# First attention: the future part of the diagonal probabilities is cleared on GpSimd, and the steps of a unit follow a table

## The chip, the core and the metric

The kernel runs on one core of one Trainium2 chip. The metric is the time of one execution on the device in microseconds, here of that one core. TensorE multiplies into PSUM, VectorE and ScalarE read PSUM and write on-chip memory (SBUF), GpSimd works in SBUF alone. Each engine runs its own program in order, and the engines meet at semaphores.

## What is computed

A model of four stages on the same tokens: a causal attention, a mixture of experts, a second attention and the experts again. The change is in the first attention only, which is, for 4 batches of 1024 tokens, 16 heads of width 16:

```
q = (x @ Wq.T).reshape(N, L, H, D).transpose(0, 2, 1, 3)     # k and v alike
q = _layernorm(q, gq, bq)                                     # over the 16 of a head
k = _layernorm(k, gk, bk)
scores = jnp.einsum('nhld,nhmd->nhlm', q, k) * SM_SCALE
causal = jnp.tril(jnp.ones((L, L), dtype=bool))
scores = jnp.where(causal, scores, NEG)
attn = jax.nn.softmax(scores, axis=-1)
out = jnp.einsum('nhlm,nhmd->nhld', attn, v)
out = out.transpose(0, 2, 1, 3).reshape(N, L, EMB)
return out @ Wo.T + bo
```

## The kernel before

**Units.** `attention_a` works in 16 units, one for each batch and group of four heads (`UNITS = B * NG`). For a unit all engines do the following steps. `qkv` multiplies normalised tokens by the weights (two halves), ScalarE copies q, k and v out and squares q and k; `spread` sums the squares on VectorE; `norm` finds 1/sqrt on ScalarE (a guess) and GpSimd (one step of refinement, `inverse_root`), and then GpSimd normalises q and k (`normalise`) and writes them with their rounding rest side by side (`build`). `stack` transposes the result on TensorE (four times 8 transposes), and ScalarE copies it out. `max` multiplies q and k of one query tile for two heads, and VectorE takes the maximum of each head: 24 such steps a unit, each two matmuls and two VectorE reductions of up to 512 columns. Four small `peak` steps for each pair of heads turn the maxima into two extra rows of q (L531 to L537), `neg` transposes q again with them (8 transposes, L704), and ScalarE copies that out. `scores` multiplies k and q again, now transposed (keys on the partitions) and with the maximum subtracted by the extra rows; ScalarE takes the exponential from PSUM into `prob`. `values` multiplies `prob` by v into one accumulator (L738), `out` copies it out on ScalarE, `back` transposes it (L747), and VectorE divides by the sum of the row. Every fourth unit `turn` and `project` finish a batch of the output; `stat`, `moments`, `xn` and `tokens` prepare the next batch of tokens.

**Twelve steps of scores.** `STEPS` lists 12 pairs of a block of 512 queries and a tile of 128 keys: tiles 0 to 3 for the first block, 0 to 7 for the second. Eight of the twelve lie on the diagonal (k = 0 to 3 and 8 to 11). There the product is 512, 384, 256 or 128 queries wide, and its first 128 queries include pairs in which the key is in the future. The kernel before adds -1e30 to these in PSUM: after the products of a step, two further bf16 matmuls of an identity with a mask (L726) are accumulated onto the first 128 columns. Of the wide steps there are two halves (one for each pair of heads), each with its own two mask matmuls; that makes 12 halves or steps with a mask in a unit and 24 mask matmuls.

**What sets the order.** One list, `ORDER`, is walked by TensorE, VectorE, ScalarE and GpSimd, each taking from each step what it has to do. `first()` writes the start, `period(n)` writes unit n. Three units are under way in period n: the scores and values of unit n, the maxima of unit n+1, and the projection, normalisation and stacks of unit n+2. `period` lays down the scores of each k with the other steps behind it, then `spread()` deals the maxima evenly over that list up to `end`, and behind `end` follow the stacks with the last two `values` and, last, `("neg", n + 1, 1)`.

**Buffers.** PSUM holds two `wide` slots of 1024 columns (tokens, qkv, stack, neg, scores, turn) that ScalarE empties, three `deep` slots of 512 columns (two for a `max`, one for `back` or `project`) that VectorE empties, and the accumulator. A step of TensorE waits until the use of its slot before has been consumed: a `max` can so start as soon as the first of the two reductions of the `max` before it is done. `prob` has three slots (`PROBS`), so the exponential of step k waits for the `values` of step k-3. GpSimd has nothing to do with `prob` in the kernel before.

Of the kernel before, what the change touches and what calls it, by code (L numbers as in the profile page):

```python
# [110 lines left out]
def attention_a(nc, c, X, tokens_in, W, dram, out, sem):  # L111
# [47 lines left out]
    def xn_tiles(b):  # L159

        return [("xn", b, t) for t in range(TB)]
# [15 lines left out]
    def stacks(u, e):  # L177

        return [("stack", u, 2 * e + i) for i in range(2)] if u < UNITS else []

    def first():

        out = []
        for x in range(2):
            out += [("tokens", 0, x), ("qkv", 0, x), ("spread", 0, x)]
        out += [("norm", 0)] + stacks(0, 0) + stacks(0, 1)
        main = [("qkv", 1, 0), ("spread", 1, 0), ("qkv", 1, 1), ("spread", 1, 1), ("norm", 1)]
        out += spread(main, maxima(0, 0), len(main)) + peak(0, 0)
        main = [("neg", 0, 0)] + stacks(1, 0)
        return out + spread(main, maxima(0, 1), len(main)) + peak(0, 1) + stacks(1, 1) + [("neg", 0, 1)]  # L190

    def period(n):

        b, g = divmod(n, NG)
        more = n + 1 < UNITS
        ahead = n + 2 < UNITS
        main = []
        for k in range(NS):
            main += scores(n, k)
            if ahead and k < 2:  # L200
                main += [("qkv", n + 2, k)]
            if ahead and k in (1, 2):
                main += [("spread", n + 2, k - 1)]
            if ahead and k == 3:
                main += [("norm", n + 2)]
            if k == 1 and n:
                main += [("back", n - 1, 1)]
            if k == TILES + 4:
                main += [("back", n, 0)]
            if k >= 2:  # L210
                main += [("values", n, k - 2)]
            if k == TILES + 1:
                main += [("out", n, 0)]
            if g == 0 and b and k in (5, 7):
                main += [("turn", b - 1, (k - 5) // 2)]
            if g == 0 and b and k in (6, 8):
                main += [("project", b - 1, (k - 6) // 2, i) for i in range(2)]
            if g == 0 and b + 1 < B and k > 1:
                main += moments(b + 1)[k - 2:k - 1]
            if g == 1 and b + 1 < B and k < 4:  # L220
                main += xn_tiles(b + 1)[2 * k:2 * k + 2]
            if g == 1 and b + 1 < B and k in (6, 7):
                main += [("tokens", b + 1, k - 6)]
            if g == 1 and k == 8:
                main += [("bias", b)]
        end = len(main)
        main += stacks(n + 2, 0) + [("values", n, NS - 2)] + stacks(n + 2, 1) + [("values", n, NS - 1), ("out", n, 1)]
        if not more:
            return main
        fill = both_maxima(n + 1)  # L230
        out = spread(main, fill, end)
        at = out.index(("peak", n + 1, 0, 3))
        later = [i for i, s in enumerate(out) if i > at and s[0] == "scores"][2]
        return out[:later] + [("neg", n + 1, 0)] + out[later:] + [("neg", n + 1, 1)]

    ORDER = moments(0) + xn_tiles(0) + first()
    for n in range(UNITS):
# [19 lines left out]
    with ExitStack() as ctx:  # L257
# [56 lines left out]
        s_bias = sem("a_bias_added")  # L314
        s_wide = sem("a_wide_slot_filled")
        s_act = sem("a_wide_slot_consumed")
        s_deep = sem("a_deep_slot_filled")
        s_dve = sem("a_deep_slot_consumed")

# [43 lines left out]
        with nc.Block() as block:  # L363
# [30 lines left out]
            def _(pool):  # L394
# [24 lines left out]
                for step in ORDER:  # L419
                    what = step[0]  # L420
                    if what == "moments" and step[1]:
                        root(step[1])
                    elif what == "norm":

                        u = step[1]
                        pool.wait_ge(s_guess, u + 1)
                        inverse_root(pool, hrstd[:], hvar[:], tmp[:])
                        pool.drain().then_inc(s_hrstd, 1)
                        for side in range(2):
                            if u == 0 and side:  # L430
# [3 lines left out]
                                continue  # L434
                            normalise(pool, side)
                            if side:
                                copied(pool, ("stack", u - 1, 3))
                            elif u > 1:
                                copied(pool, ("neg", u - 2, 1))
                            build(pool, u, side)  # L440
                            pool.drain().then_inc(s_built, 1)
                    elif what == "bias":

                        b = step[1]
                        xs = X[:, b * TB:(b + 1) * TB, :]
                        pool.wait_ge(s_xn, b + 1)
                        pool.tensor_tensor(xs, xs, bo[:].unsqueeze(1).to_broadcast([P, TB, D]), ALU.add)
                        pool.drain().then_inc(s_bias, 1)
# [188 lines left out]
            def _(pe):  # L637
                ident = c["ident"]
                pe.wait_ge(s_init, 1)
                for step in ORDER:  # L640
# [65 lines left out]
                    elif what == "scores":  # L706
# [4 lines left out]
                        diag = kt * P >= qc * QC  # L711
# [1365 lines left out]
```

## Time and profile before

| | |
|---|---|
| median of 3 runs | 4082.97 us (4077.39 to 4085.25) |
| the profiled execution | 4081.54 us |
| its span, first to last instruction | 4079.7 us |
| TensorE busy | 3499.5 us, 86% |
| VectorE / ScalarE / GpSimd busy | 2554.2 / 2217.1 / 1044.8 us |
| first attention, steady part | 103.4 to 912 us of the span |
| TensorE busy in that part | 706.9 of 808.6 us |
| VectorE / ScalarE / GpSimd busy there | 491.7 / 434.4 / 211.0 us |

The span is cut into stretches of time here, and in the first attention a stretch from one second `neg` step to the next is one period. In a timeline of TensorE a line is a run of like matmuls: its start, its length, and in brackets how long the engine had been idle before it and what ended that. Lengths of matmuls are modelled with their way through the array, so they overlap a little: what one costs is the distance from its start to the start of the next. An fp32 matmul of full precision is counted twice (x8 for four of them). Granted clock is TensorE's: 1.00 is 2.4 GHz, 0.50 is 1.2 GHz.

### The profile page before, as it was taken

The numbers are of one execution on the slowest core, as the hardware profiler recorded it, in microseconds if no ns is written. First come the engines' busy times: TensorE is split into PE (matmuls) and PEld (weight loads), VectorE is DVE, ScalarE is ACT, GpSimd is POOL, SyncE is SP. The second block draws the span as 40 slices with busy tenths as digits, with TensorE's granted clock in tenths as the row PEclk, the third lists the DMA queues.
The fourth block names the chain that finished last, engine by engine and source line by source line (L and its number), as shares of the span: only waits on it lengthen the run. The fifth ranks groups of instructions, "written<-read, shape, count | busy, mean of one in ns | idle before, by whom it ended". The sixth has DMA issues, their size and how long they took to land. (4 is left out here: it accounts for less than half of the span.)

```text
span 4079.7 us, 55078 instructions
## 1 busy us (share of the span) xinstructions
PE 3499.5 (86%) x21412; PEld 2544.7 (62%) x21412; DVE 2554.2 (63%) x4350; ACT 2217.1 (54%) x2873; POOL 1044.8 (26%) x924
## 2 busy tenths in 40 slices
PE   4888888888999999996767767777766999999998
PEld 3444454446888889996333333333323888889998
DVE  4666555654443345554999999999996443335564
ACT  1555555554322234442998899889995332224443
POOL 3322223210012201123473272363320002210121
PEclk7889998999999999998777878887777999999999
DMA  3000000001001014332000000000001001012332
GB/s 118 1 1 1 1 1 1 1 1 63 6 24 37 30 41 115 97 89 74 1 1 0 1 1 1 1 1 1 1 1 62 6 7 42 26 49 87 89 93 53
DMA packets 86805, 124.88 MB, mean 31 GB/s; under 512 B 7767, under 2 KB 73257, under 8 KB 86544
## 3 DMA queue, kind: packets, MB, share of 16 engines
q1 hardware_dynamic: 68880, 100.18, 7.3%
q0 software_dynamic: 17664, 21.17, 3.1%
q8 instruction: 170, 2.79, 0.3%
q14 instruction: 91, 0.75, 0.1%
HBM read 85.15 MB, written 42.55 MB: 31 GB/s over the span
## 5 line engine op out<-in xcount | busy, mean ns | idle before, releaser
L1846 DVE TENSOR_TENSOR b_w<-b_w 128x2048 f32<-128x2048 f32 x256 | 583.5, 2310 | 23.9 <-ACT b_w L1924 15.9
L1883 ACT ACTIVATE b_w<-b_ring 128x1024 f32<-128x1024 f32 x512 | 481.8, 1049 | 94.3 <-PE b_ring L1966 93.7
L1924 ACT ACTIVATE b_w<-b_w 128x2048 f32<-128x2048 f32 x256 | 468.1, 1898 | 1.4
L1396 ACT ACTIVATE f2hid<-f2ring 128x512 f32<-128x512 f32 (+2 forms) x256 | 132.6, 518 | 577.4 <-PE f2ring L1476 560.4
L1396 ACT ACTIVATE f1hid<-f1ring 128x512 f32<-128x512 f32 (+2 forms) x256 | 132.6, 518 | 576.6 <-PE f1ring L1476 559.5
L1954 PE MATMUL b_acc<-b_w,b_vg 128*32 128x512 f32 x2048 | 319.9, 705 | 127.8 <-DVE b_w L1846 126.7
L1314 DVE TENSOR_TENSOR f2hid<-f2hid,f2ring 128x512 f32<-128x512 f32 (+2 forms) x256 | 150.1, 586 | 439.7 <-ACT f2hid L1396 439.6
L1314 DVE TENSOR_TENSOR f1hid<-f1hid,f1ring 128x512 f32<-128x512 f32 (+2 forms) x256 | 150.1, 587 | 439.0 <-ACT f1hid L1396 438.9
L620 ACT ACTIVATE a_prob<-a_wide 128x1024 f32<-128x1024 f32 (+1 forms) x320 | 293.0, 944 | 221.5 <-PE a_wide L726 151.8
L518 DVE CUSTOM_DVE_ANT_0 a_deep<-a_deep,a_edge 128x128 f32<-128x128 f32 (+3 forms) x512 | 241.5, 514 | 218.0 <-PE a_deep L696 215.3
L1790 DVE TENSOR_SCALAR b_w<-b_w 128x2048 f32<-128x2048 f32 x256 | 324.8, 1314 | 31.0 <-ACT b_w L1883 30.6
L1476 PE MATMUL f1ring<-f1xh,f1wg 128*128 128x512 f32 (+2 forms) x1536 | 326.1, 354 | 10.6 <-DVE f1xh L1297 8.4
L1476 PE MATMUL f2ring<-f2xh,f2wg 128*128 128x512 f32 (+2 forms) x1536 | 326.1, 354 | 10.1 <-DVE f2xh L1297 7.9
L1966 PE MATMUL b_ring<-b_qT,b_kT 64*128 64x512 f32 x1024 | 237.0, 515 | 101.1 <-ACT b_w L1883 73.3
L1966 PEld LDWEIGHTS b_ring<-b_qT,b_kT 64*128 64x128 f32 x1024 | 94.4, 203 | 317.2 <-ACT b_w L1883 159.8
L1476 PEld LDWEIGHTS f1ring<-f1xh,f1wg 128*128 128x128 f32 x1536 | 250.6, 190 | 35.6 <-DVE f1xh L1297 9.3
L1476 PEld LDWEIGHTS f2ring<-f2xh,f2wg 128*128 128x128 f32 x1536 | 250.7, 190 | 35.1 <-DVE f2xh L1297 8.8
L696 PE MATMUL a_deep<-a_kT,a_qT 64*128 64x512 f32 (+3 forms) x768 | 189.3, 490 | 91.8 <-DVE a_mxp L518 45.6
L1687 POOL CAST b_stacks<-b_qk 128x256 fp32r<-128x256 f32 x64 | 141.5, 2210 | 455.6 <-DVE b_len L1776 444.2
L696 PEld LDWEIGHTS a_deep<-a_kT,a_qT 64*128 64x128 f32 x768 | 80.4, 206 | 244.1 <-DVE a_mxp L518 119.1
L521 DVE TENSOR_REDUCE a_mxp<-a_deep 128x1 f32<-128x512 f32 x256 | 164.7, 685 | 82.2 <-PE a_deep L696 80.5
L1495 PEld LDWEIGHTS f1acc<-f1wd,f1hh 128*128 128x128 f32 x1536 | 200.7, 191 | 17.0 <-DVE f1hh L1142 7.6
(342 smaller groups left out, 7017.5 us busy)
## 6 DMA issues: line engine op xcount, KB each, us to landing
X<-expert_in SPq DMA_DIRECT2D x16, 650.0 KB, 5.0
expert_in<-a_zeros SPq DMA_DIRECT2D x8, 650.0 KB, 10.4
X<-in_x SPq DMA_DIRECT2D x4, 1024.0 KB, 10.0
x_mid<-X SPq DMA_DIRECT2D x8, 512.0 KB, 3.2
f1raw_x<-in_rd SPq DMA_DIRECT2D x4, 1024.0 KB
f1raw_xf<-in_rg SPq DMA_DIRECT2D x4, 1024.0 KB, 4.9
f1raw_xf<-in_ru SPq DMA_DIRECT2D x4, 1024.0 KB, 7.0
f1raw_g<-in_rg SPq DMA_DIRECT2D x4, 1024.0 KB, 4.8
```

The costliest lines, as they stand in the source:

```text
L518: v.tensor_tensor_reduce(got, got, edge[:, CHUNK - n:], 1.0, LOWEST, ALU.add, ALU.max, peak).then_inc(s_dve, 1)
L620: s.activation(dst, src.rearrange("p (h e n) -> p h e n", h=2, e=pairs)[:, :, :, 0:n], ACT.Exp).then_inc(s_act, 1)
L696: last = pe.matmul(dslot(step, h)[:, 0:hi - lo], qT[at, u % 3, e, t * P:(t + 1) * P], kT[at, u % 3, e, lo:hi], start=True, stop=True)
L1314: v.tensor_tensor(hid[:, s % 2, 0:n], hid[:, s % 2, 0:n], slot(step)[:, QC:QC + n], ALU.mult).then_inc(free_of(step), 1)
L1396: s_eng.activation(hid[:, s % 2, 0:n], slot(step)[:, 0:n], ACT.Silu).then_inc(s_silu, 1)
L1476: last = pe.matmul(dst[:, j * QC:j * QC + n], w[:, a, cc, i * P:(i + 1) * P], xh[:, b, x, cc, first:first + n], start=(k == 0 and cc == 0) ...
L1790: v.tensor_scalar(one(m), one(m), LOG_MIN, None, ALU.max).then_inc(s_bound, 1)
L1846: v.tensor_tensor(one(m), one(m), one(m), ALU.mult).then_inc(s_wts, 1)
L1883: s.activation(w[:, m, 2 * pair:2 * pair + 2, :].rearrange("p h n -> p (h n)"), slot(at + pair), ACT.Ln, scale=SHEP_EPS ** -2).then_inc(R. ...
L1924: s.activation(one(m), one(m), ACT.Sigmoid, scale=-0.5).then_inc(s_sig, 1)
L1954: last = pe.matmul(acc[32 * h:32 * h + 32, qc, :], vg[:, u % 2, h, x, :], w[:, x, h, :], start=(x == 0), stop=(x == TB - 1))
L1966: last = pe.matmul(slot(n + e)[:, h * QC:(h + 1) * QC], kT[at, u % 2, e, x * P:(x + 1) * P], qT[at, u % 2, e, qc * QC:(qc + 1) * QC], star ...
```

## The change

All of it is in `attention_a`.

- The mask matmuls are gone. The product of a diagonal step is exponentiated as it is, and then, once the last half of the step is out, GpSimd sets the future entries of the first 128 queries of all four heads in `prob` to zero with one `affine_select` in place (128 partitions by 4 by 128), with a semaphore `s_causal`. The `values` of a diagonal step waits for it too. There are 8 selects a unit.
- `norm` on GpSimd is cut in four parts further on: `("fit", u, side, i)`, i = 0 for `normalise`, i = 1 for `build`. The instructions are the same.
- `spread()` no longer lays out a unit. A table `UNIT` of 95 letters says which kind of step comes next (m a maximum or peak, s scores, v values, q qkv, p spread and norm, w fit, k stack, n neg, b back, o out, x one of the lists of steps that belong to a batch), the same for every unit.

```diff
+    UNIT = ("mbsmxxqmsmmpqxmmsmspvsmspvmswswxvmsvmsommssmmv"
+            "msvmsxwmwsmvmsnmsbxmsvsmkmkxmvmxkmmsmmmvxxkvvo"
+            "xnx")
...
+        for kind in UNIT:
+            if kind == "x":
+                out += aside.pop(0)
+            elif kind == "b" and before:
+                out += before.pop()
+            elif line[kind]:
+                out.append(line[kind].pop(0))
+        return out
...
+                    elif what == "scores":
+
+                        u, k, x = step[1:]
+                        qc, kt = STEPS[k]
+                        n = width(k)
+                        if kt * P >= qc * QC and x == parts(k) - 1:
+                            copied(pool, step)
+                            edges = prob[:, k % PROBS, :, QC - n:QC - n + P]
+                            pool.affine_select(out=edges, in_=edges, compare_op=ALU.is_ge, fill=0.0, base=0,
+                                               pattern=[[0, HG], [1, P]], channel_multiplier=-1)
+                            pool.drain().then_inc(s_causal, 1)
...
-                                                 qT[at, u % 3, e, (qc + 1) * QC - n:(qc + 1) * QC], start=(y == 0),
-                                                 stop=not diag)
-                        if diag:
-                            for h in range(2):
-                                edge = dst[:, h * QC:(h + 1) * QC].rearrange("p (e n) -> p e n", e=pairs)[:, :, 0:P]
-                                last = pe.matmul(edge, c["identb"][:], c["mask_k"][:].unsqueeze(1).to_broadcast([P, pairs, P]),
-                                                 start=False, stop=True)
+                                                 qT[at, u % 3, e, (qc + 1) * QC - n:(qc + 1) * QC], start=True,
+                                                 stop=True)
                         last.then_inc(s_wide, 1)
...
                         copied(pe, ("scores", u, k, parts(k) - 1))
+                        if kt * P >= qc * QC:
+                            pe.wait_ge(s_causal, 2 * TILES * u + qc * TILES + kt % TILES + 1)
```

The order of TensorE at the start of period 7, before (L704 is `neg` of the unit before the seam, L720 `scores`, L726 mask, L696 `max`, L674 `qkv`):

```order
L704 MATMUL a_wide<-ident,a_qs 128x128 x8
L720 MATMUL a_wide<-a_qT,a_kT 128x512 x2
L726 MATMUL a_wide<-mask_k,identb 128x128 x2
L720 MATMUL a_wide<-a_qT,a_kT 128x512 x2
L726 MATMUL a_wide<-mask_k,identb 128x128 x2
L696 MATMUL a_deep<-a_kT,a_qT 128x128 x2
L674 MATMUL a_wide<-a_wqkv,a_xnT 128x192 x8
L696 MATMUL a_deep<-a_kT,a_qT 128x256 x2
L720 MATMUL a_wide<-a_qT,a_kT 128x384 x2
L726 MATMUL a_wide<-mask_k,identb 128x128 x2
```

The same place now (L731 `neg`, L723 `max`, L770 `back`, L746 `scores`, L701 `qkv`):

```order
L731 MATMUL a_wide<-ident,a_qs 128x128 x8
L723 MATMUL a_deep<-a_kT,a_qT 128x128 x2
L770 MATMUL a_deep<-ident,a_oT 128x128 x4
L746 MATMUL a_wide<-a_qT,a_kT 128x512 x2
L723 MATMUL a_deep<-a_kT,a_qT 128x256 x2
L701 MATMUL a_wide<-a_wqkv,a_xnT 128x192 x8
L723 MATMUL a_deep<-a_kT,a_qT 128x384 x2
L746 MATMUL a_wide<-a_qT,a_kT 128x512 x2
L723 MATMUL a_deep<-a_kT,a_qT 128x512 x4
L701 MATMUL a_wide<-a_wqkv,a_xnT 128x192 x8
L723 MATMUL a_deep<-a_kT,a_qT 128x128 x2
```

A `max` and the `back` of the unit before now stand between the `neg` and the first `scores`, the second half of the scores stands behind the first `qkv`, and the masks are gone.

TensorE at the end of period 6, before (L685 `stack`, L738 `values`):

```order
L738 MATMUL a_acc<-a_prob,a_vg 32x384 x4
L685 MATMUL a_wide<-ident,a_qs 128x128 x8
L685 MATMUL a_wide<-ident,a_ks 128x128 x8
L738 MATMUL a_acc<-a_prob,a_vg 32x256 x4
L685 MATMUL a_wide<-ident,a_qs 128x128 x8
L685 MATMUL a_wide<-ident,a_ks 128x128 x8
L738 MATMUL a_acc<-a_prob,a_vg 32x128 x4
L704 MATMUL a_wide<-ident,a_qs 128x128 x8
```

And now (L712 `stack`, L761 `values`; the `stack` before the first row here stands between two `max` as well):

```order
L712 MATMUL a_wide<-ident,a_ks 128x128 x8
L723 MATMUL a_deep<-a_kT,a_qT 128x384 x2
L761 MATMUL a_acc<-a_prob,a_vg 32x512 x4
L723 MATMUL a_deep<-a_kT,a_qT 128x512 x2
L712 MATMUL a_wide<-ident,a_qs 128x128 x8
L723 MATMUL a_deep<-a_kT,a_qT 128x512 x2
L746 MATMUL a_wide<-a_qT,a_kT 128x128 x4
L761 MATMUL a_acc<-a_prob,a_vg 32x384 x4
L712 MATMUL a_wide<-ident,a_ks 128x128 x8
L761 MATMUL a_acc<-a_prob,a_vg 32x256 x4
L761 MATMUL a_acc<-a_prob,a_vg 32x128 x4
L731 MATMUL a_wide<-ident,a_qs 128x128 x8
```

Of the 24 `max` steps none stood in this last part before, behind the last `scores`. Now four stand between the first and the last of the four stacks, and behind the last `max` there are a `scores`, a `values`, a `stack` and two more `values` before the `neg`.

GpSimd from one unit's k (L340 to L344 `normalise`, L356 to L361 `build`) to the next unit's `norm` (L75), before:

```order
L340 TENSOR_TENSOR a_qk<-a_qk,a_hrstd 128x512
L342 TENSOR_TENSOR a_qk<-a_qk,a_gain 128x512
L344 TENSOR_TENSOR a_qk<-a_qk,a_shift 128x512
L356 CAST a_ks<-a_qk 128x32x16 [waits a_wide_slot_consumed]
L357 CAST a_ks<-a_qk 128x32x16
L361 TENSOR_TENSOR a_ks<-a_qk,a_ks 128x32x16
L75 TENSOR_TENSOR a_tmp<-a_hrstd 128x64 [waits a_head_rstd_guessed]
```

And now (L352 to L356 `normalise`, L368 to L373 `build`):

```order
L352 TENSOR_TENSOR a_qk<-a_qk,a_hrstd 128x512
L354 TENSOR_TENSOR a_qk<-a_qk,a_gain 128x512
L356 TENSOR_TENSOR a_qk<-a_qk,a_shift 128x512
L368 CAST a_ks<-a_qk 128x32x16 [waits a_wide_slot_consumed]
L369 CAST a_ks<-a_qk 128x32x16
L373 TENSOR_TENSOR a_ks<-a_qk,a_ks 128x32x16
L466 AFFINE_SELECT a_prob<-a_prob 128x4x128 [waits a_wide_slot_consumed] x8
L75 TENSOR_TENSOR a_tmp<-a_hrstd 128x64 [waits a_head_rstd_guessed]
```

Eight selects (four of the last diagonal steps, four of the first of the next unit) stand between one unit's `build` and the next unit's `norm`; each waits for ScalarE's exponential.

## Rows read from the trace of the kernel before

**Rows 1.** Windows of the first attention: TensorE, its weight loads, VectorE, ScalarE, GpSimd busy; clock.

```profile
103.40:315.10 211.70, 182.52 (x1230) 97.09 (x1228) 131.49 (x403) 113.14 (x154) 59.86 (x70) 0.90 0.00 1
315.10:531.20 216.10, 189.59 (x1285) 104.17 (x1281) 133.26 (x409) 115.44 (x157) 59.89 (x70) 0.92 0.00 1
531.20:752.40 221.20, 195.60 (x1284) 106.19 (x1281) 133.83 (x409) 115.68 (x157) 59.87 (x70) 0.89 0.00 1
752.40:912.00 159.60, 139.18 (x982) 72.91 (x978) 93.09 (x288) 90.10 (x115) 31.33 (x35) 0.96 0.00 1
```

**Rows 2.** Waits of TensorE from 100 to 912 us: total, times, longest.

```profile
PE a_deep L696 <- DVE a_mxp L521: 39.0, 62, 1.3
PE a_deep L696 <- DVE a_mxp L518: 38.1, 67, 1.8
```

**Rows 3.** Timeline of TensorE in period 7: start, length, instructions, idle before.

```profile
483.16 1.09 PE L704 MATMUL a_wide<-ident,a_qs 128*128 128x128 f32 x8
...
485.51 0.51 PE L720 MATMUL a_wide<-a_qT,a_kT 64*128 64x512 f32 x2 [0.62 <-ACT a_qT L611]
485.95 0.29 PE L726 MATMUL a_wide<-mask_k,identb 128*128 128x128 bf16 x2
486.16 0.33 PE L696 MATMUL a_deep<-a_kT,a_qT 64*128 64x128 f32 x2
486.42 2.87 PE L674 MATMUL a_wide<-a_wqkv,a_xnT 128*128 128x192 f32 x16
...
496.52 0.33 PE L696 MATMUL a_deep<-a_kT,a_qT 64*128 64x128 f32 x2 [0.80 <-DVE a_mxp L521]
...
498.04 0.51 PE L696 MATMUL a_deep<-a_kT,a_qT 64*128 64x512 f32 x2 [0.58 <-DVE a_mxp L518]
499.33 0.58 PE L696 MATMUL a_deep<-a_kT,a_qT 64*128 64x256 f32 x2 [0.79 <-DVE a_mxp L521]
499.84 1.94 PE L738 MATMUL a_acc<-a_prob,a_vg 128*32 128x512 f32 x8
...
523.66 0.39 PE L726 MATMUL a_wide<-mask_k,identb 128*128 128x256 bf16 x2
523.99 1.07 PE L738 MATMUL a_acc<-a_prob,a_vg 128*32 128x512 f32 x8
...
531.17 1.09 PE L704 MATMUL a_wide<-ident,a_qs 128*128 128x128 f32 x8
```

**Rows 4.** Two windows of period 7, columns as in Rows 1.

```profile
495.90:499.30 3.40, 1.44 (x10) 0.71 (x10) 2.97 (x10) 1.51 (x2) 0.00 (x0) 1.00 0.00 0
499.30:502.70 3.40, 3.37 (x16) 1.32 (x16) 2.29 (x8) 0.00 (x0) 0.00 (x0) 0.50 0.00 0
```

**Rows 5.** VectorE's groups in period 7: busy us, mean ns, idle before.

```profile
L521 DVE TENSOR_REDUCE a_mxp<-a_deep 128x1 f32<-128x512 f32 x16 | 10.3, 685 | 5.0 <-PE a_deep L696 5.0
L518 DVE CUSTOM_DVE_ANT_0 a_deep<-a_deep,a_edge 128x512 f32<-128x512 f32 x8 | 5.4, 714 | 0.3
L518 DVE DVE_READ_ACCUMULATOR2_ANT a_mxp<- 128x1 f32 x32 | 4.5, 140 | 0.0
L518 DVE CUSTOM_DVE_ANT_0 a_deep<-a_deep,a_edge 128x128 f32<-128x128 f32 x8 | 2.2, 318 | 8.9 <-PE a_deep L696 8.9
```

**Rows 6.** Timeline of GpSimd at the start, in unit 0 and in period 7.

```profile
4.32 0.29 POOL L398 TENSOR_SCALAR_AFFINE_SELECT a_edge<-a_edge 128x128 f32<-128x128 f32 x1 [0.19 <-issue]
...
39.01 1.51 POOL L340 TENSOR_TENSOR a_qk<-a_qk,a_hrstd 128x512 f32<-128x512 f32 x1 [0.24 <-issue]
...
504.33 0.29 POOL L75 TENSOR_TENSOR a_tmp<-a_hrstd 128x64 f32<-128x64 f32 x1 [35.27 <-ACT a_hrstd L602]
...
506.20 1.06 POOL L340 TENSOR_TENSOR a_qk<-a_qk,a_hrstd 128x512 f32<-128x512 f32 x1 [0.24 <-issue]
...
510.23 0.61 POOL L356 CAST a_qs<-a_qk 128x512 fp32r<-128x512 f32 x1
...
518.45 1.29 POOL L361 TENSOR_TENSOR a_ks<-a_qk,a_ks 128x512 f32<-128x512 f32 x1
```

More of the change, by code:

```diff
@@ L179, in stacks, with fits @@
         return [("stack", u, 2 * e + i) for i in range(2)] if u < UNITS else []
+    def fits(u):
+        return [("fit", u, side, i) for side in range(2) for i in range(2)]
     def first():
@@ L185, in first @@
             out += [("tokens", 0, x), ("qkv", 0, x), ("spread", 0, x)]
-        out += [("norm", 0)] + stacks(0, 0) + stacks(0, 1)
-        main = [("qkv", 1, 0), ("spread", 1, 0), ("qkv", 1, 1), ("spread", 1, 1), ("norm", 1)]
-        out += spread(main, maxima(0, 0), len(main)) + peak(0, 0)
+        out += [("norm", 0)] + fits(0) + stacks(0, 0) + stacks(0, 1)
+        main = [("qkv", 1, 0), ("spread", 1, 0), ("qkv", 1, 1), ("spread", 1, 1), ("norm", 1)] + fits(1)
+        out += spread(main, maxima(0, 0), len(main) - 4) + peak(0, 0)
@@ L189, in first, with beside @@
         main = [("neg", 0, 0)] + stacks(1, 0)
         return out + spread(main, maxima(0, 1), len(main)) + peak(0, 1) + stacks(1, 1) + [("neg", 0, 1)]
+    UNIT = ("mbsmxxqmsmmpqxmmsmspvsmspvmswswxvmsvmsommssmmv"
+            "msvmsxwmwsmvmsnmsbxmsvsmkmkxmvmxkmmsmmmvxxkvvo"
+            "xnx")
+    def beside(b, g):
+        at = [[] for _ in range(NS)]
+        if g == 0 and b:
+            for k, step in ((4, ("turn", b - 1, 0)), (5, ("project", b - 1, 0, 0)), (6, ("project", b - 1, 0, 1)),
+                            (6, ("turn", b - 1, 1)), (7, ("project", b - 1, 1, 0)), (8, ("project", b - 1, 1, 1))):
+                at[k].append(step)
+        if g == 0 and b + 1 < B:
+            for k, step in enumerate(moments(b + 1)):
+                at[k + 1].append(step)
+        if g == 1 and b + 1 < B:
+            for i, step in enumerate(xn_tiles(b + 1)):
+                at[i // 2].append(step)
+            at[6].append(("tokens", b + 1, 0))
+            at[8].append(("tokens", b + 1, 1))
+        if g == 1:
+            at[9].append(("bias", b))
+        return at
@@ L192, in period @@
     def period(n):
-        b, g = divmod(n, NG)
         more = n + 1 < UNITS
         ahead = n + 2 < UNITS
[L197 to L234, printed above, removed]
+        line = {
+            "s": [step for k in range(NS) for step in scores(n, k)],
+            "v": [("values", n, k) for k in range(NS)],
+            "o": [("out", n, x) for x in range(2)],
+            "b": [("back", n, 0)],
+            "m": both_maxima(n + 1) if more else [],
+            "n": [("neg", n + 1, e) for e in range(PAIRS)] if more else [],
+            "q": [("qkv", n + 2, x) for x in range(2)] if ahead else [],
+            "p": [("spread", n + 2, 0), ("spread", n + 2, 1), ("norm", n + 2)] if ahead else [],
+            "w": fits(n + 2) if ahead else [],
+            "k": stacks(n + 2, 0) + stacks(n + 2, 1),
+        }
@@ L236, in attention_a @@
+        before = [[("back", n - 1, 1)]] if n else [[]]
+        aside = beside(*divmod(n, NG))
+        out = []
+        for kind in UNIT:
[6 more added lines that the diff above has]
+        return out
     ORDER = moments(0) + xn_tiles(0) + first()
@@ L316, in attention_a @@
         s_act = sem("a_wide_slot_consumed")
+        s_causal = sem("a_future_probs_cleared")
         s_deep = sem("a_deep_slot_filled")
@@ L428, in _ @@
                         pool.drain().then_inc(s_hrstd, 1)
-                        for side in range(2):
-                            if u == 0 and side:
+                    elif what == "fit":
+                        u, side, i = step[1:]
+                        if u == 0 and side:
+                            if i:
                                 pool.wait_ge(s_first, 1)
                                 pool.drain().then_inc(s_built, 1)
-                                continue
+                        elif i == 0:
                             normalise(pool, side)
+                        else:
                             if side:
@@ L710, in _ @@
                         n = width(k)
-                        diag = kt * P >= qc * QC
                         pairs = PAIRS // parts(k)
```

## The prediction

> **What bounds the kernel now.** I read the windows first. In the first attention TensorE is busy 182.5 of 211.7 us, 189.6 of 216.1, 195.6 of 221.2 and 139.2 of 159.6, and VectorE, next in line, 131 to 134 us of each of the first three [rows 1]. So TensorE sets the pace, yet it idles 808.6 - 706.9 = 101.7 us of this part. The second thing to see there is the granted clock: 0.90, 0.92, 0.89 and 0.96. The clock has the two levels 1.2 and 2.4 GHz, so a mean of 0.90 is 20% of the time at 1.2 GHz, and work done there takes twice as long. The loss is about 0.10 x 211.7 + 0.08 x 216.1 + 0.11 x 221.2 + 0.04 x 159.6 = 69 us.
>
> Who causes the idle time stands in the waits: 39.0 + 38.1 = 77 us of it is a `max` of TensorE that waits for VectorE to empty a deep slot [rows 2]. The timeline of period 7, 48.0 us from one `neg` to the next, shows how that comes about and what it brings. Three waits of 0.80, 0.58 and 0.79 us lie within 3.6 us, because `spread` and `back` stand on VectorE between two `max`; right behind them the products of a `values` take 1.94 us where the same eight take 1.07 us later [rows 3]. The windows of these stretches tell the same: TensorE is busy 1.44 of 3.4 us while VectorE is busy 2.97, and the 3.4 us after that are granted 0.50 [rows 4]. At the end of the period the picture is turned round: there is no `max` behind the last `scores`, and VectorE idles (8.9 us before the narrow maxima of the next period [rows 5]). So each period has a stretch in which VectorE paces TensorE and one in which it has nothing to do, and the first of them also costs clock.
>
> **Part 1, the masks.** From the start of a narrow pair of mask matmuls to the next instruction are 486.16 - 485.95 = 0.21 us, of a wide pair 523.99 - 523.66 = 0.33 us [rows 3]. A unit has eight narrow pairs and four wide ones: 8 x 0.21 + 4 x 0.33 = 3.0 us, times 16 units 48 us at full clock. They lie on TensorE's own path. Where VectorE paces, their time would turn into waiting, but they are in the scores, and only some of those stand in such a stretch. I take 48.
>
> **Part 2, the selects.** No row shows a select of 128 x 512. The nearest rows are a select of 128 x 128, 0.29 us, and a one-input copy of 128 x 512 in the same 16-element rows, 0.61 us; the top is a two-input operation of 128 x 512 at 1.29 us [rows 6]. I take the copy's, 0.65 us, since the select too reads one input and writes as many elements. Eight are 5 us a unit; GpSimd is busy 60 us in a batch of four units of some 215 [rows 1], so its throughput is no limit. What counts is the way from exponential to `values`: 0.8 us longer with its semaphores. Against TensorE's order the tightest places are the `values` of k = 1, with a `values`, two `scores` and a `max` (about 2.4 us) between its last `scores` and itself against 0.85 + 0.8 us, and the last one of the unit, with 2.4 us of `values` and `stack` against 0.6 + 0.8. Both are covered; at 1.29 us for a select the first would wait some 0.3 us a unit, 5 us in all, and that is the upper bound unless selects queue behind something.
>
> They do queue behind one thing. GpSimd's `norm` and its parts take from 504.33 to 519.74 = 15.4 us in a row [rows 6], the last four selects of a unit stand behind them, and so does the `stack` of k. Before, they ended 531.17 - 519.74 = 11.4 us ahead of the period's last `neg`. By the walk below the guess arrives 16 us into a period, GpSimd is through at 31.7, and TensorE comes to the `stack` of k at 33.0 and to `values` 8 at 34.3. Nothing waits, with 1.3 us in hand. I cost it at zero; if `norm` is 2 us later than I think, it costs 0.7 us a unit, 10 us in all.
>
> The Trainium skill, page "GPSIMD Engine Reference", section "Specifications", says that GpSimd shares its SBUF interfaces with VectorE and contends with VectorE instructions that have two SBUF inputs; that speaks against moving work there. The trace shows such a case: the same product took 1.51 us at 39.01, where VectorE ran `normalise` too, and 1.06 us in period 7 [rows 6]. By that ratio a select would be 0.9 us instead of 0.65 and the sum 0 to 5 us worse; in a period the maxima read PSUM and one SBUF operand, so I leave it out.
>
> **Part 3, the order.** I walked period 7 in the new order by hand, each step of TensorE at its start-to-start distance at full clock and each maximum at VectorE's duration. A `max` can start when the first reduction of the pair before is done, so after a 512-wide `max` the next can start about 0.7 + 0.14 us after VectorE begins the pair [rows 5]. The waits that remain are 0.3 and 0.9 us at the two `max` after the first `qkv` (three in a row with one `scores` between them), 0.5 and 0.45 us at the two after the second `qkv`, 0.5 us at the first `max` of the second pair of heads, and 0.1 to 0.2 us at the `neg` behind the last peaks: about 3.0 us. `back` now stands ahead of the first `qkv`, whose 2.8 us [rows 3] let VectorE catch up, and both `spread` fall where TensorE has `qkv` or `values` to do. The half of the scores that waited 0.62 us for the copied `neg` [rows 3] has work ahead of it. At the end the maxima run beside the stacks. Period 7 was 48.0 us, of it 5.3 idle and 3.4 at half clock (1.7 lost), so 41 us of work; less 3.0 of masks 38, plus 3.0 of waits 41.
>
> The walk leaves out small waits for ScalarE and semaphores; of the 5.3 us in period 7, 1.2 were of that kind. With these a period has 4.2 us of idle time instead of 101.7 / 16 = 6.4: 2.2 x 16 = 35 us gained.
>
> The clock is the larger and less certain term. It fell after clusters like 0.80 + 0.58 + 0.79. In the new order the densest cluster is 0.3 + 0.9. In the periods in which VectorE also normalises the next batch's tokens (`xn`, one in four) it comes to about 1.5 us, and there I expect the clock to go on falling. I take 20 of the 69 us as left: 49 gained.
>
> **The sum.** 48 + 35 + 49 = 132. Idle time within stretches of half clock has been counted in both terms; I put a tenth of the 138 us at half clock as idle (the window of rows 4 at 0.50 has 1%, but longer falls run into waits again), and half of that, 7 us, comes off. A further 5 us go for period 14, which has no `qkv` and no `stack` but all 24 maxima, so that VectorE sets its pace. That leaves 120. The profiled execution had 4081.5 us (span 4079.7), so 3961.5; on the scale of the runs' median, which is 1.4 us higher, 3963. What follows the attention starts when it ends and is moved as it is.
>
> **The rivals.**
> - Masks only. The waits move to the new clusters, the clock falls once a period as it does now, and only the 48 us are saved: 4035. For it speaks that the 1.2 us of waits round the first three `max` are not far from the 2.2 that made the clock fall, and that a fall there would strike a `qkv` of 2.8 us. Against it, VectorE has 13 us more of each period to spread its work over.
> - All of it. The clock stays at 2.4 GHz and the small waits go: 48 + 54 + 69 - 7 - 5 = 159, 3924.
> - GpSimd late. `norm` and its parts hold the selects 8 to 11 and the k stack back by 3 us a unit: 16 x 3 = 48 us off the gain, 4011.
> - Slower: GpSimd becomes the bound. The place is its program between `build` of k and the next `norm`. A unit costs it 15.4 us plus eight selects, and 53 us are there (the mean period). Above (53 - 15.4) / 8 = 4.7 us a select it is slower than before; at 5 us, and with the bias addition of every fourth unit, 16 x 3.5 = 55 us more, 4138. Rows speak against it by a factor of seven, but none has this operation with an outer stride.
> - Nothing that can be measured: a loss at the select of about the masks' worth, with the waits only moved, 4080.
>
> **How the numbers follow.** The forecast, between 3935 and 3995, gets 0.62; all of it 0.08; masks only 0.15; GpSimd late 0.08; nothing 0.03; slower 0.04. The range from 3925 to 4036 leaves out less than 0.1 above and about half of the case below, some 0.17 in all with the ends of the others. A measurement of this kernel can tell about 0.2%, 8 us, from no change. Faster by more: 0.62 + 0.08 + 0.15 + 0.08 = 0.93. Same 0.03, slower 0.04.
>
> **What would show it.** Right: the mask group is gone; periods of 41 to 44 us without batch work, 50 to 53 with `project`; TensorE waits for VectorE under 50 us in all; clock 0.96 or more over the attention; selects of 0.5 to 0.8 us, and hardly a wait of `values` for them. Wrong: a clock of 0.9 with waits of 1 us round the first maxima (masks only); waits of TensorE for GpSimd at `stack` or `values` (late); GpSimd busy over 40 us a period (slower). If the selects are much longer than 1.3 us, part 2 has failed first.

## The result and the profile after

The changed kernel takes 3945.9 us (median of 4 runs, 3943.9 to 3947.7) against 4084.1 us of the kernel before: 0.966 of it, 95% interval 0.964 to 0.968. That is 138 us less; 3963 was forecast, with a range of 3925 to 4036. The profiled execution took 3943.95 us.

The page, its span and first part:

```profile
span 3942.2 us, 54680 instructions
PE 3388.5 (86%) x21028; PEld 2512.1 (64%) x21028; DVE 2567.0 (65%) x4350; ACT 2215.9 (56%) x2873; POOL 1127.5 (29%) x1052
```

384 matmuls and their weight loads are gone, 128 instructions of GpSimd are new. The difference lies in the first attention. The window from the second `neg` of unit 0 to that of unit 15 (15 periods, columns as in [rows 1]), which was 796.3 us long before, is now:

```profile
99.00:764.50 665.50, 590.77 (x4326) 346.59 (x4323) 504.09 (x1507) 423.60 (x568) 287.56 (x365) 0.96 0.00 1
```

It is 131 us shorter. The waits of TensorE in that window (total in us, times, longest; in each line the step that waited, then the engine and tile that it waited for):

```profile
PE a_deep L723 <- DVE a_mxp L545: 37.7, 63, 0.9
PE a_wide L731 <- DVE a_qs L564: 16.4, 7, 4.2
PE a_deep L723 <- DVE a_mxp L548: 11.6, 19, 0.8
PE a_wide L712 <- POOLq L457: 5.5, 7, 0.8
```

Against [rows 2] the wait for the maxima has gone from 77 to 49 us, and its longest from 1.8 to 0.9. Two of these waits are new. The `stack` of k waits for GpSimd, at most 0.8 us at a time. And `neg` waits for the last peak step, seven times, up to 4.2 us; four of the seven, of 3.3 us three times and 4.2 once, make up 14 of the 16 us. What lies behind that is in no step of the prediction. Timelines of GpSimd, VectorE and TensorE at the end of period 5:

```profile
357.30 0.63 POOL L466 TENSOR_SCALAR_AFFINE_SELECT a_prob<-a_prob 128x512 f32<-128x512 f32 x1 [4.17 <-ACT a_prob L647]
358.12 4.52 POOL L474 TENSOR_TENSOR X<-X,a_bo 128x2048 f32<-128x2048 f32 x1 [0.18 <-issue]
```

```profile
358.04 0.18 DVE L560 TENSOR_SCALAR a_qs<-a_mx 128x16 fp32r<-128x16 f32 x1
358.30 4.38 DVE L562 TENSOR_TENSOR a_neglo<-a_qs,a_mx 128x16 f32<-128x16 f32 x1
362.75 0.18 DVE L564 TENSOR_SCALAR a_qs<-a_neglo 128x16 fp32r<-128x16 f32 x1
```

```profile
358.90 0.86 PE L761 MATMUL a_acc<-a_prob,a_vg 128*32 128x256 f32 x16
363.08 1.94 PE L731 MATMUL a_wide<-ident,a_qs 128*128 128x128 f32 x8 [3.33 <-DVE a_qs L564]
```

GpSimd finishes the last select of the unit at 357.9 and starts the bias addition (L474), 4.5 us on 2048 columns. VectorE's small two-input subtraction (L562, 16 columns), 0.18 us elsewhere, begins 0.2 us later and ends when the bias addition does. `neg` waits 3.33 us for it, and the clock falls behind this idle time:

```profile
357.00:361.70 4.70, 2.75 (x36) 2.15 (x32) 4.46 (x5) 2.65 (x4) 4.22 (x2) 1.00 0.01 3
361.70:371.90 10.20, 8.82 (x32) 7.63 (x33) 3.32 (x12) 2.04 (x2) 0.94 (x1) 0.50 0.00 0
```

These are the two windows about the end of period 5: TensorE is busy 2.75 of 4.7 us, then 10.2 us pass at 1.2 GHz. The same hold of 4.38 us stands in the trace at each of the four bias additions.

### The profile page after: what moved, and what is told of

The parts are those of the page before. It is cut to its first block and busy times, and to the rows that moved or that the text cites. A ratio compares the mean times of both kernels' runs of the same rounds, so it can differ in the third digit from the quotient of the medians.

```text
span 3942.2 us, 54680 instructions
## 1 busy us (share of the span) xinstructions
PE 3388.5 (86%) x21028; PEld 2512.1 (64%) x21028; DVE 2567.0 (65%) x4350; ACT 2215.9 (56%) x2873; POOL 1127.5 (29%) x1052
## 5 line engine op out<-in xcount | busy, mean ns | idle before, releaser
L723 PE MATMUL a_deep<-a_kT,a_qT 64*128 64x512 f32 (+3 forms) x768 | 170.5, 440 | 64.9 <-DVE a_mxp L545 45.4
L1518 PEld LDWEIGHTS f2acc<-f2wd,f2hh 128*128 128x128 f32 x1536 | 200.7, 191 | 17.1 <-DVE f2hh L1165 7.6
L1977 PEld LDWEIGHTS b_acc<-b_w,b_vg 128*32 128x32 f32 x2048 | 44.3, 116 | 261.3 <-DVE b_w L1869 220.4
```

The source lines that it names most:

```text
L1518: last = pe.matmul(acc[:, g % 2, t * D:(t + 1) * D], hh[:, s % 2, a, t * P:(t + 1) * P], w[:, part, i, :], start=(i == 0 and k == 0 and t ...
L1977: last = pe.matmul(acc[32 * h:32 * h + 32, qc, :], vg[:, u % 2, h, x, :], w[:, x, h, :], start=(x == 0), stop=(x == TB - 1))
```

## The experiments

All times are medians, of 4 runs or more except where said, and each ratio is to the kernel before on the same chip. The kernel before took 4080.0 to 4081.4 us there, against 4084.1 in the comparison above, so a difference between two experiments is good to some 4 us; where it matters, the windows of the profiled executions are given beside it. For every kernel the 15 periods are split in three: idle time is length less busy time, the loss of clock is busy time times (1 - granted clock), and what is left, busy time times clock, is about the work at full clock. The clock is rounded to 0.01, so the last two are good to some 3 us. Window lines have their columns as in [rows 1].

### The masks back in the new order

```diff
-                            pool.affine_select(out=edges, in_=edges, ...)
+                                last = pe.matmul(edge, c["identb"][:], c["mask_k"][:]...)
```

> The changed kernel's order with the mask matmuls back and no select on GpSimd. If a mask costs what I summed ahead (3.0 us a unit, 48 in all), 3994. If it also holds up the scores matmul ahead of it (start of a 512-wide scores pair to the mask 0.43 us, to another 64-row matmul 0.34), 3.9 us a unit, 63 in all: 4009. In both the clock of the attention stays near 0.96; if the clock gain came from the masks' going and not from the order, it falls back to 0.91 and the time is over 4030.

Measured: 3963.6 us (3960.3 to 3973.7), 0.972 (0.971 to 0.974). Lower than either number: with all its masks the new order alone saves 117 us, and taking them out adds only 18 (the windows of the 15 periods: 682.2 and 665.5 us, 17 apart; by the ratios 0.972 and 0.966 it would be 26).

```profile
97.90:780.10 682.20, 628.08 (x4687) 358.17 (x4685) 499.45 (x1507) 425.68 (x568) 211.24 (x245) 0.99 0.00 1
```

The clock is 0.99 here, better than the 0.96 of the changed kernel, and TensorE idles 54 us against 75. So the work that the masks cost is in the window, 622 us against 567, but the changed kernel gives two fifths of these 55 us back as idle time and another third as clock.

### The select in the old order, and no mask at all

```diff
-                        if diag:
-                            for h in range(2):
-                                last = pe.matmul(edge, c["identb"][:], c["mask_k"][:]...)
+                            pool.affine_select(out=edges, in_=edges, ...)
```

> The kernel before with the masks taken out and the select on GpSimd put in, order unchanged. By the forecast's parts: 4084 less 48 to 63 us, 4021 to 4036, with the clock still near 0.91 and the waits of TensorE for VectorE at 77 us or more. Rival: most of the gain of the change is the masks', then below 3990. Rival: selects queue behind norm, which the old order starts later; then values wait for GpSimd and it is over 4060.

Measured: 4085.6 us (4073.9 to 4093.1, 10 runs), 1.001 (1.000 to 1.002). None of the three expectations holds as written: nothing is saved, and the clock, expected near 0.91, is 0.84 over the 15 periods. 4060 was named as the sign that `values` wait for GpSimd, but the waits show that they do not; TensorE's wait for the maxima is 86 us. To separate GpSimd's part, the next kernel leaves the mask out and puts nothing in its place:

```diff
-                        if diag:
-                            for h in range(2):
-                                last = pe.matmul(edge, c["identb"][:], c["mask_k"][:]...)
```

> The kernel before with the mask matmuls left out and nothing in their place, so that future keys count in the softmax; the time is read for TensorE's work alone. Theory: in the old order the 62 us of full-clock work that the masks took come back as idle time and lost clock whatever GpSimd does, so 4070 to 4090 as with the select. Rival: the select's way over GpSimd ate them in e2_select_old_order; then 4020 to 4040 here.

Measured: 4078.0 us (4073.2 to 4084.3, 10 runs), 0.999 (0.998 to 1.000). The windows of the two, the select first:

```profile
103.40:909.60 806.20, 684.66 (x4326) 365.95 (x4324) 504.80 (x1507) 421.85 (x568) 286.69 (x365) 0.84 0.00 1
```

```profile
102.70:898.00 795.30, 671.43 (x4326) 361.76 (x4324) 494.80 (x1507) 421.81 (x568) 210.62 (x245) 0.86 0.00 1
```

GpSimd is not what ate the masks' time; with the select the time is 8 us longer than with nothing, which the two intervals do not quite part. The clock is 0.84 and 0.86 instead of 0.91. The timeline of TensorE in period 7 of the kernel without masks shows how:

```profile
496.33 0.33 PE L696 MATMUL a_deep<-a_kT,a_qT 64*128 64x128 f32 x2 [0.80 <-DVE a_mxp L521]
...
497.85 0.50 PE L696 MATMUL a_deep<-a_kT,a_qT 64*128 64x512 f32 x2 [0.91 <-DVE a_mxp L518]
499.14 0.58 PE L696 MATMUL a_deep<-a_kT,a_qT 64*128 64x256 f32 x2 [0.79 <-DVE a_mxp L521]
499.65 1.93 PE L732 MATMUL a_acc<-a_prob,a_vg 128*32 128x512 f32 x8
```

It is the cluster of [rows 3], and the middle wait has grown from 0.58 to 0.91: by 0.33, the price of the wide pair of masks that stood there. At this place VectorE paces TensorE, and the work taken from TensorE has become waiting, one for one. Not all of the idle time comes at the maxima. Over the 15 periods it grows by 24 us; the waits for the maxima make 11 of it (76.3 to 87.6), and 8 are the `scores` that wait until ScalarE has copied the `neg`, 10.2 us in all in the kernel before and here:

```profile
PE a_wide L719 <- ACT a_qT L611: 17.9, 27, 0.8
```

The rest of the 57 us of work is lost by the clock, 94 us instead of 63. Why the clock falls by so much is not shown by this run.

### One step of the old order moved

```diff
         for k in range(NS):
+            if k == 0 and n:
+                main += [("back", n - 1, 1)]
             main += scores(n, k)
-            if k == 1 and n:
-                main += [("back", n - 1, 1)]
```

> The kernel before with one step moved: back of the unit before stands ahead of the first scores instead of behind the second, so that VectorE has it out of the way before the first maxima. Theory: it takes the middle out of the cluster of waits (0.80, 0.58, 0.79 us) behind which the clock fell in most periods; clock of the attention from 0.91 to 0.94 or more, 4084 less 20 to 35: about 4055. Rival: the falls come from the maxima alone, clock stays 0.91 and the time within 8 us of 4084.

Measured: 4050.3 us (4046.2 to 4060.9), 0.993 (0.992 to 0.995). The window of its 15 periods:

```profile
98.70:864.10 765.40, 669.92 (x4687) 367.14 (x4685) 488.63 (x1507) 423.62 (x568) 210.87 (x245) 0.95 0.00 1
```

The idle time has hardly changed (95 against 100 us), the clock went from 0.91 to 0.95, and 30 us are saved in all. So the sum of the waits does not set the clock. The trace of the kernel before has the same in two of its own periods; the first idles 4.8 us at a clock of 0.87, the second 7.2 us at 1.00:

```profile
213.90:264.80 50.90, 46.12 (x309) 24.27 (x304) 31.07 (x95) 27.82 (x39) 13.42 (x17) 0.87 0.01 1
315.10:373.30 58.20, 51.02 (x357) 30.19 (x353) 35.89 (x116) 29.89 (x41) 15.09 (x18) 1.00 0.00 1
```

What the moved step changed is how the waits are bunched. Instead of 0.80, 0.58 and 0.79 us, 2.2 in all, period 7 has these three, 1.6 in all, and the `values` between them takes 1.07 us and not 1.94:

```profile
480.90 0.39 PE L696 MATMUL a_deep<-a_kT,a_qT 64*128 64x256 f32 x2 [0.79 <-DVE a_mxp L521]
481.21 1.07 PE L738 MATMUL a_acc<-a_prob,a_vg 128*32 128x512 f32 x8
482.78 0.50 PE L696 MATMUL a_deep<-a_kT,a_qT 64*128 64x512 f32 x2 [0.50 <-DVE a_mxp L518]
...
484.07 0.44 PE L696 MATMUL a_deep<-a_kT,a_qT 64*128 64x384 f32 x2 [0.29 <-DVE a_mxp L521]
```

Periods 2, 3, 6, 7, 10, 11 and 13 all run at 1.00 now, where they had 0.84 to 0.97; the others, most of them with batch work, still have 0.83 to 0.97. This one step is a quarter of what the new order brings. The other moves of the new order (the maxima beside the stacks, the second half of the `scores` behind `qkv`, both `spread`) were not tried one by one, and which of them bring the other 87 us is not shown.

### The bias addition, moved and split

```diff
-        if g == 1:
-            at[9].append(("bias", b))
+        if g == 2:
+            at[2].append(("bias", b))
```

> The changed kernel with the bias addition on GpSimd (4.5 us, once in four units) moved from the end of unit 1 of a batch to the third x of unit 2, where VectorE has maxima and no two-input instruction on SBUF. Theory: the 4.4 us of VectorE's L562 in every fourth unit are the bias addition's doing; they fall to 0.2, the four waits of 3.3 to 4.2 us at neg go and with them falls of the clock: 15 us of idle time and about 10 of clock, 3921. Rival: VectorE is late there because the unit also has xn tiles; then L562 stays long or another step is late, 3946.

Measured: 3921.7 us (3917.0 to 3925.5), 0.961 (0.960 to 0.963).

```diff
-                        pool.tensor_tensor(xs, xs, bo[:].unsqueeze(1).to_broadcast([P, TB, D]), ALU.add)
+                        for t in range(TB):
+                            pool.tensor_tensor(xs[:, t], xs[:, t], bo[:], ALU.add)
```

> The changed kernel with the bias addition left in its place but cut into eight instructions of 256 columns. Theory A: VectorE's two-input instruction is held for one GpSimd instruction at a time, so L562 takes at most 0.8 us and most of the 25 us come back: 3925. Theory B: it is held as long as GpSimd has such work queued, so L562 stays near 4.4 us: 3946.

Measured: 3919.1 us (3916.3 to 3925.2), 0.961 (0.960 to 0.963). VectorE's subtraction in this last kernel (shortest, median, longest in ns), its window, and the same subtraction in the changed kernel:

```profile
L563 DVE TENSOR_TENSOR a_neglo<-a_qs,a_mx x32: 179/181/597, 74.0 to 735.2; 128x16 f32<-128x16 f32 x32
```

```profile
98.00:735.80 637.80, 575.65 (x4326) 336.38 (x4325) 490.56 (x1507) 424.14 (x569) 291.63 (x393) 0.99 0.00 1
```

```profile
L562 DVE TENSOR_TENSOR a_neglo<-a_qs,a_mx x32: 179/181/4381, 74.9 to 763.6; 128x16 f32<-128x16 f32 x32
```

Both edits bring the 25 us, as expected (24 and 27; the window of the split is 28 us shorter), and with the split the longest hold is 0.6 us, less than one piece of 0.73 us. More pieces were queued behind it, so VectorE's instruction is held by one GpSimd instruction at a time. TensorE's idle time goes from 75 to 62 us and the clock from 0.96 to 0.99. Both kernels beat the changed one by 0.6 to 0.7%.

In the kernel before the same subtraction takes at most 0.55 us in the 15 periods. Whether the order or the select makes the collision was tested with the masks back and the bias addition split:

> e1_masks_new_order with the bias addition split as in e4_bias_split. In e1 VectorE's L550 was never longer than 0.3 us, since without selects GpSimd does the bias addition earlier. Theory: the collision with the bias addition is made by the select ahead of it, so the split brings nothing here: 3958 to 3966; the masks' going is then worth 40 us in the new order (to 3919), of which the collision gave back 25. Rival: the split itself saves something everywhere: 3940.

Measured: 3963.6 us (3960.6 to 3967.1), 0.971 (0.969 to 0.973), the same as without the split. In e1_masks_new_order, where GpSimd has no selects, the subtraction never takes long:

```profile
L550 DVE TENSOR_TENSOR a_neglo<-a_qs,a_mx x32: 179/180/313, 73.9 to 778.6; 128x16 f32<-128x16 f32 x32
```

So the collision comes with the select: the bias addition stands behind the unit's last select in GpSimd's program, and that select is released just when the last peaks are due. In period 1 the bias addition starts at 180.05 us in the changed kernel and the last peak's subtraction at 180.23; without selects they start at 174.37 and 183.99. With the collision out of the way the masks' going is worth 3963.6 - 3919.1 = 44 us in the new order, instead of 18.

### How much room the select has

```diff
+                            for _ in range(3):
+                                pool.drain()
                                 pool.affine_select(out=edges, in_=edges, ...)
```

> The changed kernel with each select done three times (2.4 us instead of 0.8), result the same. Throughput of GpSimd: 15.4 + 8 x 2.4 = 35 us of a period of 41 to 49, so by throughput alone nothing changes: 3946. Latency: sel 1, 2, 3 follow each other and push norm back by 5 us, the last four selects stand behind norm and each costs 1.6 us more, so TensorE waits 3 us at the k stack and 4 to 5 us at the values of the end: about 7 us a unit, 110 in all: 4055.

Measured: 4036.0 us (2 runs), 0.989 (0.987 to 0.991): 90 us more than the changed kernel, not the 110 expected, but by the way of latency and not of throughput. Of the 90, 69 lie in the 15 periods (734.3 against 665.5 us) and most of the rest in the last unit. TensorE's waits in the 15 periods:

```profile
PE a_acc L763 <- POOLq L470: 56.9, 51, 2.0
PE a_deep L725 <- DVE a_mxp L547: 37.2, 62, 0.9
```

`values` (L763) waits 51 times for a select, while GpSimd is busy 440 of 734 us. One select takes 635 ns in the changed kernel; at three of them it is on the path.

### Two attempts at a better table

> The changed kernel with only periods 14 and 15 laid out by the old spread. Theory: period 14 is paced by VectorE (24 maxima, no qkv, no stacks) and the table bunches the maxima at its start; evenly dealt the clock stays up and it takes 35 instead of 41 us: 3940. Rival: VectorE's 31 us of work set the period whatever the order: 3946.

Measured: 3946.2 us (3943.9 to 3947.5), 0.967 (0.965 to 0.969); the edit was a function for periods 14 and 15 that is the old `period` without its steps for unit n + 2. The rival's number holds: period 14 took 41.7 us instead of 41.1. Its reason does not, as the next run shows. With the bias addition moved as well:

> The changed kernel with the bias addition moved as in e3_bias_moved, and periods 14 and 15 laid out by the old spread of maxima instead of the table, which has no qkv and stacks to put between them. If both add up: 25 us for the bias, and period 14, 41.1 us with 10.7 idle and half its time at half clock, comes to 35: 3915.

Measured: 3927.4 us (3923.1 to 3931.7), 0.962 (0.961 to 0.964), if anything slower than the 3921.7 with the move alone. There the table's period 14 had come down to 37.1 us by itself, at a clock of 0.91 instead of 0.75; with the old spread it takes 42.9 us at 0.72. What made it long in the changed kernel was the half clock behind the bias addition, not the table.

```diff
-    UNIT = ("mbsmxxqmsmmpqxmmsmspvsmspvmswswxvmsvmsommssmmv"
+    UNIT = ("mbsmxxqmsmpqxmmsmspvmsspvmswsmwxvmsvmsommssmmv"
```

> e4_bias_split with a table in which one maximum of the first third stands behind the second qkv instead of ahead of it, and the next ones move back by one until behind the scores of k = 4. Theory: VectorE paces TensorE in this stretch only (waits 0.49, 0.85, 0.46, 0.62 us of a period); the wait of 0.85 goes and the period is 1 us shorter: 3919 less 15, 3904. Rival: the waits come back later in the period, since VectorE is as busy, 3919.

Measured, on top of the split: 3921.2 us (3917.2 to 3925.6), 0.961 (0.959 to 0.962), against 3919.1. The wait of 0.85 us is gone from its place and back in others; the waits of TensorE:

```profile
PE a_deep L724 <- DVE a_mxp L546: 30.0, 69, 0.9
PE a_deep L724 <- DVE a_mxp L549: 20.5, 46, 0.8
PE a_wide L732 <- DVE a_qs L565: 9.8, 14, 1.0
```

60.3 us in all, where the split with the table as it is has 37.6 + 11.8 + 3.0 = 52.4. The wait of `neg` for the last peak (L732) has gone from 3.0 to 9.8 us: a maximum that is done later makes the peaks later.

## Why the forecast held, and where it did not

The account of the 15 periods. The window of the kernel before for it, columns as in [rows 1]:

```profile
103.40:899.70 796.30, 696.41 (x4687) 375.62 (x4685) 490.99 (x1507) 424.28 (x568) 210.96 (x245) 0.91 0.00 1
```

All in us:

| kernel | length | idle | clock loss | work at full clock |
|---|---|---|---|---|
| before | 796 | 100 | 63 | 634 |
| before, no mask | 795 | 124 | 94 | 577 |
| before, select for masks | 806 | 122 | 110 | 575 |
| new order, masks | 682 | 54 | 6 | 622 |
| changed kernel | 666 | 75 | 24 | 567 |
| changed, bias split | 638 | 62 | 6 | 570 |

The table covers 15 of the 16 periods that the prediction summed.

**The sum** was 120 us and 138 were measured. Its three parts were added as if they were independent, and that is the step that failed. By their sizes they look fair: 48 for the masks, 35 for idle time, 49 for the clock, against 67, 25 and 39 in the table. But which edit brings them is another matter. By the runs the order alone brings 117 us where the sum had 84 for it, less the 12 taken off at the end, and the masks' going brings 18 on top where the sum had 48. The one is 45 too small and the other 30 too large; that they nearly cancel, and the total lands 18 us from the measured one, is luck. The 67 us of work are not all the masks' either: with and without them it differs by 55 us in the new order and 57 in the old. The other 12 go with the order (more under part 1).

**Part 1, the masks.** Mis-sized in two ways. The mask costs more than the 0.21 us to the next instruction: from a scores pair of 512 to its mask are 485.95 - 485.51 = 0.44 us [rows 3], while in the changed kernel a `values` starts 0.33 us behind such a pair:

```profile
342.32 0.39 PE L746 MATMUL a_wide<-a_qT,a_kT 64*128 64x512 f32 x2
342.65 1.06 PE L761 MATMUL a_acc<-a_prob,a_vg 128*32 128x512 f32 x8
```

So a mask also makes the scores ahead of it dearer by 0.1 us, unless what follows them would do so anyway. Other steps of 128 rows by 128 columns do it too; in the kernel before `qkv` starts 0.43 us behind a `max` pair of 512:

```profile
491.40 0.51 PE L696 MATMUL a_deep<-a_kT,a_qT 64*128 64x512 f32 x2
491.83 2.87 PE L674 MATMUL a_wide<-a_wqkv,a_xnT 128*128 128x192 f32 x16
```

Summed as e1_masks_new_order expected, that makes 3.9 us a unit and 63 in all, where 48 had been taken. Measured it is less than 3.9 and more than 3.0. Period 7 ran at a clock of 1.00 with one step of the old order moved (e5_back_first) and with the masks in the new order; in the changed kernel it is busy 36.5 us (its window stands under part 3):

```profile
466.40:511.90 45.50, 40.96 (x308) 22.33 (x304) 30.24 (x95) 27.56 (x39) 13.41 (x17) 1.00 0.00 1
```

```profile
414.80:458.20 43.40, 39.79 (x308) 22.24 (x304) 32.20 (x95) 28.07 (x39) 13.43 (x17) 1.00 0.00 1
```

The masks' going takes 39.8 - 36.5 = 3.3 us of work off it, which is 53 in 16 units, and the order alone 41.0 - 39.8 = 1.2. The 55 and 57 of the table are 3.7 and 3.8 a period, within the rounding of its clocks. Why the same matmuls take 1.2 us less in the new order is not shown. And the sentence "They lie on TensorE's own path" was true of a part of them only. The old order gives all of it back (4085.6 and 4078.0 against 4080 and 4081); the new one keeps 44 us if the bias addition is out of the way and 18 if not. The rival "masks only" was priced 4035 by the same error: the masks alone are worth nothing, and 4080, the price of the rival "nothing that can be measured", which I had kept for a loss at the select, is what they give.

**Part 2, the select.** 0.65 us was taken, 0.635 measured. The 1.3 us in hand at the `stack` of k were not there in half of the periods: that step waited seven times, 5.5 us in all, up to 0.8. No `values` waited for GpSimd in the 15 periods. The rule on shared SBUF interfaces, of the Trainium skill's page "GPSIMD Engine Reference", section "Specifications", was weighed for GpSimd's side alone and put at 0 to 5 us. It was VectorE's side that counted. The trace agrees with the rule that instructions with two SBUF inputs contend (4.38 us for one of 0.18, against GpSimd's two-input addition of 4.52), and the price is 25 us. I had asked what the select meets, and not what the select moves: the bias addition had to be followed too, as an instruction of GpSimd that is queued behind the select.

**Part 3, the order.** The walk of period 7 gave 41 us, 42.2 with the small waits; it took 40.8. The waits that it named stand where it put them; the window and the timeline of TensorE in period 7:

```profile
409.30:450.10 40.80, 36.52 (x283) 20.86 (x281) 30.88 (x95) 28.13 (x40) 18.50 (x25) 1.00 0.01 1
```

```profile
415.67 0.50 PE L723 MATMUL a_deep<-a_kT,a_qT 64*128 64x512 f32 x2 [0.50 <-DVE a_mxp L545]
417.02 0.50 PE L723 MATMUL a_deep<-a_kT,a_qT 64*128 64x512 f32 x2 [0.85 <-DVE a_mxp L545]
...
442.78 1.06 PE L712 MATMUL a_wide<-ident,a_ks 128*128 128x128 f32 x8 [0.77 <-POOLq L457]
```

The first two were forecast as 0.3 and 0.9; the two behind the second `qkv`, 0.5 and 0.45, took 0.46 and 0.61. The idle time of the period is 40.8 - 36.5 = 4.3 us, where 3.0 of named and 1.2 of small waits were forecast. That is near in sum, but 0.77 of it is the `stack` of k that waits for GpSimd, which had been put at zero. The work is 36.5 us where 38 were forecast: 0.3 of the 1.5 are the masks' higher price and 1.2 come with the order, which the walk did not have. That the period came out at the 41 of the walk is chance.

**The clock.** 20 us were to be left and 24 were, but not where I said. The periods with `xn` tiles, where the clock was to go on falling, have 0.98 to 1.00; four fifths of what is lost in the changed kernel lies in the four periods behind a bias addition, and with the bias addition split 6 us are left. That the place of the waits, and not only their sum, makes the clock fall is shown by e5_back_first: one step moved, idle time nearly the same, clock from 0.91 to 0.95.

Of the signs named ahead, the mask group that is gone, the clock of 0.96 and the selects of 0.6 us came out. The periods are a little shorter than forecast, 40.4 to 40.8 us without batch work (41 to 44 named) and 48.7 to 50.3 with `project` (50 to 53 named); only those behind a bias addition took 41 to 46 us. TensorE's waits for VectorE were to be under 50 us in all and are 37.7 + 16.4 + 11.6 = 65.7: 49 for the maxima, and the 16 at `neg` that the prediction did not have.

## What to carry to other kernels

Work taken from the engine that looks busiest is worth its time only where that engine sets the pace; in a stretch in which another engine hands it its buffers it becomes waiting, and here the clock of TensorE fell with it: 57 us of work gone from the old order brought 3 us. Deal the paced steps over the whole period first, then take work out. When an engine's program gets a new step, follow the long instructions queued behind it: they move, and what they meet at the new place has to be costed.

## What the hardware showed that was not expected

- A VectorE instruction with two SBUF inputs and 16 columns took up to 4.38 us while GpSimd ran one two-input addition of 4.52 us; with that addition in eight pieces it took at most 0.60 us.
- 100 us of idle time went with a clock of 0.91 and 95 us with 0.95, in kernels that differ by the place of one step a period. With 54 us of idle time it was 0.99.
- Behind a pair of 64-row matmuls of 512 columns a step of 128 rows by 128 columns (a mask, `qkv`) started after 0.43 to 0.44 us, in the kernel before, and a further 64-row pair after 0.34. Why is not shown.
- 57 us of TensorE's work at full clock were taken out of the old order and the time stayed at 0.999 (0.998 to 1.000) of what it was.
